# Four triangle layers on one core: the second layer's blocks with the channel innermost

## The reference, cut to what matters

```
xn = layernorm(groupnorm(x))
left  = (xn @ w_left.T)  * mask * sigmoid(xn @ w_lgate.T)      # rounded to bfloat16
right = (xn @ w_right.T) * mask * sigmoid(xn @ w_rgate.T)      # rounded to bfloat16
og    = sigmoid(xn @ w_ogate.T)
out   = einsum('bikh,bjkh->bijh', left, right)                 # rounded to bfloat16, then float32
x     = x + (layernorm(out) * og) @ w_out.T
```

## Time and profile before

| | |
|---|---|
| Runs | 2094.15 us median of 3 |
| The profiled execution's own time | 2098.47 us |
| Its span, first to last instruction | 2096.6 us |
| Mean granted TensorE clock | 0.958 |
| Second layer's projection, first to last L601 | 692.8 to 955.0 us |
| Second layer's triangle, first L1057 to the end of the last L1069 | 964.55 to 1029.95 us |

### The profile page before, as it was taken

The page is one execution under the profiler, slowest core; times in us unless marked ns, Lnnn a source line. Parts: engine busy times, 40 slices in busy tenths (PEclk is TensorE's granted clock), DMA queues, the critical chain, the costliest instruction groups (busy, mean ns, idle before and its releaser), DMA issues. The chain is left out here.

```text
span 2096.6 us, 40996 instructions
## 1 busy us (share of the span) xinstructions
PE 1779.0 (85%) x10389; PEld 1041.3 (50%) x10389; DVE 1326.5 (63%) x2984; ACT 1372.8 (65%) x2541; POOL 1006.1 (48%) x916
## 2 busy tenths in 40 slices
PE   0899997797998899995599799789799999699776
PEld 0445454685554445453255477633344444588433
DVE  7566666124763677776977388466377778344675
ACT  0577876355996788874499666477577787344554
POOL 0267678003991577776699300089222223000599
PEclk9999999798999999998899899999899999899999
DMA  7357876774996355546399666089547777845599
GB/s 325 123 181 235 246 231 218 268 290 170 366 367 232 101 188 173 187 149 253 135 349 366 242 217 209 32 316 375 193 150 232 234 236 216 296 179 222 187 397 377
DMA packets 326949, 496.17 MB, mean 237 GB/s; under 512 B 22828, under 2 KB 188463, under 8 KB 320439
## 3 DMA queue, kind: packets, MB, share of 16 engines
q1 hardware_dynamic: 326838, 494.93, 68.4%
HBM read 285.12 MB, written 197.13 MB: 230 GB/s over the span
## 5 line engine op out<-in xcount | busy, mean ns | idle before, releaser
L804 POOL TENSOR_TENSOR lo<-xn,hi 128x512 f16<-128x512 f32 x192 | 224.0, 1167 | 374.1 <-DVE hi L736 230.6
L601 PE MATMUL ps<-w_heads,hi 64*128 64x256 f16 x3072 | 294.0, 274 | 10.2 <-DVE sig L750 4.5
L1112 ACT ACTIVATE O<-ps 128x512 f32 (+1 forms) x144 | 151.8, 1054 | 190.5 <-PE ps L1033 190.5
L750 DVE SCALAR_TENSOR_TENSOR sig<-ps,largest,sig 128x512 f32<-128x512 f32 x256 | 180.8, 746 | 142.8 <-ACT sig L664 141.9
L664 ACT ACTIVATE sig<-ps,largest 128x512 f32<-128x512 f32 x384 | 246.2, 692 | 30.7 <-PE ps L601 28.6
L645 ACT ACTIVATE zs<-ps,shift 128x512 f32<-128x512 f32 x192 | 131.9, 687 | 191.4 <-PE ps L569 188.5
L1349 POOL TENSOR_TENSOR shared<-O,out_rs 128x128 f32<-128x128 f32 (+1 forms) x112 | 76.4, 684 | 370.8 <-DVE out_rs L1249 369.8
L601 PEld LDWEIGHTS ps<-w_heads,hi 64*128 64x128 f16 x3072 | 153.9, 95 | 167.1 <-DVE sig L750 67.3
L1397 PEld LDWEIGHTS ps<-ident,shared 128*128 128x128 f32 (+1 forms) x1024 | 120.0, 133 | 225.5 <-issue 96.4
L1397 PE MATMUL ps<-ident,shared 128*128 128x128 f32 (+1 forms) x1024 | 160.8, 282 | 75.6 <-POOL shared L1349 48.9
L601 PE MATMUL ps<-w_heads,lo 64*128 64x256 f16 x1536 | 213.5, 273 | 0.0
(11 more groups left out here) (164 smaller groups left out, 3724.3 us busy)
## 6 DMA issues: line engine op xcount, KB each, us to landing
shared<-left_right SPq DMA_DIRECT2D x34, 2048.0 KB, 12.0
shared<-gate SPq DMA_DIRECT2D x224, 256.0 KB, 4.6
gate<-gates SPq DMA_DIRECT2D x96, 512.0 KB, 2.9
x_dram<-shared SPq DMA_DIRECT2D x192, 256.0 KB, 4.3
shared<-x_dram SPq DMA_DIRECT2D x192, 256.0 KB, 4.7
xs<-x_dram SPq DMA_DIRECT2D x64, 512.0 KB, 4.2
left_right<-stage SPq DMA_DIRECT2D x64, 448.0 KB, 6.0
left_right<-shared SPq DMA_DIRECT2D x64, 448.0 KB, 5.7
```

The source lines that it names most:

```text
L601: last = pe.matmul(PAIR[row][:, g, kb * S:kb * S + S], tokens[half, q % 8, at:at + P], k["w_heads"][half, part, :], start=(step == 0), sto ...
L750: dve.scalar_tensor_tensor(dst, pair(row, 1), k["largest"][:, 1:2], factor, ALU.mult, ALU.mult).then_inc(pair_read.sem, 1)
L804: pool.tensor_tensor(lo[:, q % 8, :], xn[:, q % 2, :], hi[:, q % 8, :], ALU.subtract).then_inc(c["lo_done"].sem, 1)
L1112: act.activation(o_of(ch), ps[h % 4 // 2][:, h % 2, :].rearrange("p (b g i) -> p b g i", b=2, g=2), ACT.Copy).then_inc(c["o_copied"].sem, 1)
```

## The change

The order inside a block becomes (i h): the row outside, the channel inside. Three functions change.

- In `mask_rows` one instruction of 1024 elements becomes two of 512, one for each row, each waiting for its own row. It reads the 16 channels of a group from `sig` as neighbours and writes them as 16 neighbours. `lr_done` counts up by one after each.
- In `triangle`, for the bfloat16 layer alone, the tile `packed` and its semaphore are gone from use. Both the moving and the stationary operand of L1033 are read straight from the blocks, with one bfloat16 every 16 elements, that is every 32 bytes.
- VectorE's program of that stage is only the spreads of the odd channels.

The stage tiles, the DMAs and the loads keep their sizes and places, and the other three layers keep their instructions.

```diff
@@ -789,13 +789,14 @@
                 if q % SCH == 0:
                     pool.wait_ge(c[f"lr_out{b}"].sem, c[f"lr_out{b}"](i * 16 * SEG_PARTS))
                     pool.wait_ge(c[f"first_out{b}"].sem, c[f"first_out{b}"](i * 64))
-                pool.wait_ge(c["pair_read"].sem, c["pair_read"](m * 2 + 2))
-                slot, at = 2 * q % 4, q % SCH * ROWS
-                product = sig[:, slot:slot + 2, :].rearrange("p r (c e) -> p c e r", c=4)
                 by_g = k["mask"][:].rearrange("p g b i -> p (g b) i")
-                mk = by_g[:, :, bass.ds(m * ROWS, ROWS)].unsqueeze(2).to_broadcast([P, 4, P, ROWS])
-                rows = stage[b].rearrange("p g b l n (h i) -> p (g b) (l n h) i", h=HG)[:, :, :, at:at + ROWS]
-                pool.tensor_tensor(rows, product, mk, ALU.mult).then_inc(c["lr_done"].sem, 2)
+                for row in range(ROWS):
+                    pool.wait_ge(c["pair_read"].sem, c["pair_read"](m * 2 + row + 1))
+                    at = q % SCH * ROWS + row
+                    product = sig[:, (2 * q + row) % 4, :].rearrange("p (c x h) -> p c x h", c=4, h=HG)
+                    mk = by_g[:, :, bass.ds(m * ROWS + row, 1)].unsqueeze(3).to_broadcast([P, 4, P // HG, HG])
+                    dst = stage[b].rearrange("p g b l n (i h) -> p (g b) (l n) i h", h=HG)[:, :, :, at, :]
+                    pool.tensor_tensor(dst, product, mk, ALU.mult).then_inc(c["lr_done"].sem, 1)
 
             def low_part(i, q):
                 m = i * BODY + q
@@ -964,7 +965,7 @@
     with ExitStack() as ctx:
         left, right = blocks[:, 0], blocks[:, 1]
         stays = turns == 1
-        packed = ctx.enter_context(nc.sbuf_tensor(f"packed{n}", [P, RING, 2, S], low))
+        packed = None if rounded_first else ctx.enter_context(nc.sbuf_tensor(f"packed{n}", [P, RING, 2, S], low))
         rounded = ctx.enter_context(nc.sbuf_tensor(f"rounded{n}", [P, 4, 2 * S], BF16)) if rounded_first else None
         right_t = ctx.enter_context(nc.sbuf_tensor(f"right_t{n}", [P, 2, 2, S], F32)) if turned else None
         block = ctx.enter_context(nc.Block())
@@ -974,6 +975,8 @@
 
         def rows_of(block, s, h):
 
+            if rounded_first:
+                return block[:, s].rearrange("p b s (i h) -> p b (s i) h", h=HG)[:, :, :, h]
             return block[:, s].rearrange("p b s (h i) -> p b s h i", h=HG)[:, :, :, h, :]
 
         def rounded_of(slot):
@@ -1022,12 +1025,13 @@
                 ch = channel(t, s, h)
                 if turned:
                     pe.wait_ge(c["tr_copied"].sem, c["tr_copied"](ch + 1))
-                else:
+                elif not rounded_first:
                     pe.wait_ge(c["packed"].sem, c["packed"](ch + 1))
                 pe.wait_ge(c["o_copied"].sem, c["o_copied"](ch - 3))
                 for jb in range(2):
                     for kb in range(2):
                         stationary = (right_t[:, h % 2, kb, jb * P:jb * P + P] if turned
+                                      else rows_of(right, s, h)[:, kb, jb * P:jb * P + P] if rounded_first
                                       else packed[:, h % RING, kb, jb * P:jb * P + P])
                         moving = rows_of(left, s, h)[:, kb]
                         last = pe.matmul(ps[h % 4 // 2][:, h % 2, jb * S:jb * S + S], stationary,
@@ -1069,11 +1073,8 @@
                 dve.tensor_copy(o_of(ch), rounded_of(ch % 4)).then_inc(c["o_stored"].sem, 1)
 
             if rounded_first:
-                for ch in range(H):
-                    pack(ch // (2 * HG), ch // HG % 2, ch % HG)
-                    if ch >= 2 and ch % 2 == 1:
-                        spread_out(ch - 2)
-                spread_out(H - 1)
+                for ch in range(1, H, 2):
+                    spread_out(ch)
             else:
                 with dve.Fori(0, turns) as t:
                     for s in range(2):
@@ -1116,7 +1117,7 @@
         c["lr_out1"].advance(16 * SEG_PARTS)
         for s in range(2):
             c[f"lr_in{s}"].advance(32 * (turns - 1 + s))
-    for name in ("packed", "tri_done", "o_copied") + (("tr_done", "tr_copied") if turned else ()):
+    for name in ("tri_done", "o_copied") + (() if rounded_first else ("packed",)) + (("tr_done", "tr_copied") if turned else ()):
         c[name].advance(H)
     for name in ("o_stored", "o_moved") if rounded_first else ():
         c[name].advance(H // 2)
```

## The result

The changed kernel takes 2144.75 us, the median of 4 runs (2142.99 to 2146.87), against 2093.87 us, the median of 4 runs of the kernel before (2092.66 to 2095.32). The ratio is 1.0249, with a 95% interval of 1.0236 to 1.0262: slower by 50.9 us. The forecast was 2091.5 us in a range of 2087 to 2114. It failed, and so did the range.

The account below looks back on a forecast made before the run. It took the turn shared by DVE and POOL as the triangle's bound, TensorE after the change. From the median 2094.15 us, -2.7 us for the triangle and 0 for the mask gave about 2091.5 us, range 2087 to 2114.

Parts of the forecast that it names:

- What bounds the kernel: Second layer's triangle: DVE and POOL copies take turns; without packs 1.60 us per two channels, at most 5.5 us less.
- I take 0.83 ns, half the speed of now: L1033's strided reads: 0.215 us a matmul, TensorE becomes the bound, 2.7 us less; chance 0.40.
- the far end of my bounds: Highest bound for TensorE's strided read at L1033, from ACT's write L1112: 1.73 ns a column, 0.44 us a matmul.
- the milder form: Rival at L1033: 1.04 ns a column, +7.5 us, 2101.6; with one shared read path +18 us, 2112; chance 0.18.
- the break-even: Triangle: from 0.91 ns a column on, 192 matmuls take 44.3 us and the stage ends as before.
- Each column costs a fetch as slow as ACT's strided write: Rival at L1033: 1.73 ns a column, 0.44 us a matmul from the first channel on, +49 us, 2143; chance 0.13.
- or over 1.81, for then a strided read costs more than the packs: Sign of being wrong: the triangle's period per pair of channels exceeds 1.81 us.
- The weight loads: TensorE's loads of the stationary operand: double to about 0.2 us, still fit beside a matmul of 0.215.
- The first 16 channels: Triangle's start: 13.8 us of TensorE, done at 978.3, covered by the load landing at 984.1.
- The mask: POOL's two instructions of 512 for one of 1024: about 0.1 us loss at the projection's end, taken as 0.
- The dear form: Rival: POOL's mask halves cost up to 1278 ns each, 0.5 us a step, +4.5 us at the projection's end; chance 0.05.
- the tail: Projection's end, where POOL has no gap: mask period 3.12 us, against 3.11 before.

Follow-up runs that it names:

- the last experiment: Channel innermost in the right blocks only, moving operand in its old runs, nothing packed, mask in three instructions, against the kernel before: 2087.96 us, ratio 0.9973.
- the packs above: VectorE's packs in the changed kernel with the right, stationary operand packed again from every 16th element: 2141.07 us, one run.
- the sweep: Changed kernel with TensorE's operand steps varied by group of 16 channels, products not the reference's; two kernels, one run each: 2126.34 and 2115.72 us.

## Why the prediction was wrong

**What bounds the kernel.** Right, as the last experiment shows. With the packs gone and TensorE at full speed the stage is bounded by the turn of DVE and POOL, not by PE's return from 31 us of idle time. I had put the period at 1.60 us and the gain at 5.5 us; they are 1.575 us and 5.9 us. That the copies "run one after the other" is too strong, though: apart they take 772 + 1082 ns, 1.85 us for the pair, so they overlap in part. In the changed kernel itself this bound never showed.

**The step that failed** is "I take 0.83 ns, half the speed of now". The measured cost is 1.83 ns a column, 2.2 times that and a little over the far end of my bounds, 1.73 ns. I had chosen by the nearest read row, VectorE's jumping read at 1.04 ns (L1238), and took it for a pace at which SBUF serves any reader. It isn't. (The rows give 1.10 ns for that pace rather than 1.04, which moves the milder form by 2 us and decides nothing. Likewise the break-even lies at 0.90 ns a column, not 0.91.) VectorE at this kernel's own distance needs 1.1 ns for an element (the packs above), and TensorE needs 1.77 ns for every 16 bytes of the moving operand. The row was sound for its engine and said nothing of the other. That 1.73 ns, a ScalarE write, lies so near the measured value may be chance; no run tests a common cause.

**The rival that came true** is "Each column costs a fetch as slow as ACT's strided write". It had its place (L1033), its course (from the first channel on, through the cover of the loads) and nearly its price: 0.44 us a matmul against 0.468. That the total agrees as closely, +49 us and 2143 against a measured 50.9 and 2144.75, is in part luck: the triangle lost 56.2 us and not 49, and the projection's 3.2 us and the difference between executions took some of it back. I gave it 0.13 and left it out of the range. Two ends of a bound that lie four times apart, with nothing of TensorE between them, did not carry a value in the middle with 0.40, nor a range that ended at the milder forms. My own test in the text, "or over 1.81, for then a strided read costs more than the packs", came out at 3.74 us.

**The weight loads** were to double, to 0.2 us. They take 149 ns, against 104, and are hidden, as said. Of TensorE's time they make 0.008 us a matmul (0.468 against 0.460 with the right operand packed).

**The first 16 channels** were to be covered by group 1's load up to 0.30 us a matmul. At 0.468 they aren't, so all 256 matmuls count. That was right as a condition, and enters the rival's sum.

**The mask.** I took 0 for the projection, and "Each first half can start a row earlier, which no other engine waits for" was wrong: undoing that wait alone costs 2.8 us. The dear form (+4.5) did not come: two instructions take 2.07 us together, as one did. In the tail I was right, the pairs are 3.13 us apart.

**The sum with the measured terms:** 2098.47 + 56.2 for the triangle, - 3.2 for the projection and + 0.5 behind it is 2151.97. The profiled 2144.44 is 7.5 us below it, the 5.6 and 2.1 us of stages that are alike. On the medians, 2093.87 + 53.5 is 2147.4, against 2144.75.

## What to carry to other kernels

A strided operand must be priced on the engine and the side that reads it. Here the same distance of 32 bytes costs TensorE's stationary operand next to nothing, VectorE twice its time, and TensorE's moving operand four times its time at the full clock (0.46 us against 0.109), so choose the layout in which the moving operand lies together and let the stationary one be scattered. Where the nearest rows for an unknown cost are of other engines and lie far apart, the far end is a case of its own weight, above all when it decides the sign. And before a copy is taken out because an engine waits for it, ask what the engine that reads behind it gets instead.

## What the runs showed of the hardware that was not expected

- TensorE's moving read: 0.43 ns a column for neighbours and 0.44 at a step of 4 bytes, at a granted clock of 1.00; 0.88 at 8, 1.77 at 16, 1.80 at 32 and 1.68 at 64. At steps of 8 and 32 bytes it is the same at a granted clock of 1.00 and of 0.50, where neighbours go from 0.109 to 0.213 us a matmul; at 64 only 0.50 was granted. That 64 bytes are cheaper than 32 stays open.
- While TensorE worked without a pause on such reads, its granted clock was 0.50 (1.2 GHz) throughout. In the sweep it was 1.00 in 986 to 988, when the first of them ran, 0.91 in 988 to 991 and 0.50 from 991 on. With a dense matmul between each two it stayed there.
- GpSimd's write of single bfloat16 elements 32 bytes apart: 2578 ns for 512, against 1048 in runs of 16.
- Copies of VectorE and GpSimd that run side by side without a pause took 1676 and 1684 ns, one pair in 1.575 us, against 772 and 1082 in the changed kernel, where they seldom meet.
